# AdaLN attention and MLP block: maxima turned by VectorE, q and k split by POOL, residuals added by TensorE

## The reference, cut to what matters

```python
def _stablemax3_s(x):
    pos = 1.0 + x * (1.0 + 0.5 * x * (1.0 + x / 3.0))
    neg = 1.0 / (1.0 - x * (1.0 - 0.5 * x * (1.0 - x / 3.0)))
    return jnp.where(x >= 0, pos, neg)
...
attn = jnp.einsum('bhsd,bhtd->bhst', q, k) * scale
logits = logits - jnp.max(logits, axis=axis, keepdims=True)
s = _stablemax3_s(logits); return s / jnp.sum(s, axis=axis, keepdims=True)
...
h = _layernorm(x) * (1 + ca) + sa
x = x + ga * (attn(h) @ w_out.T + b_out)
h = _layernorm(x) * (1 + cb) + sb
x = x + gb * mlp(h)      # 128 -> 512 -> 512 -> 128, relu, weights 1 or -1
```

## Time and profile before

| | |
|---|---|
| median of 3 runs (lowest to highest) | 790.41 us (789.8 to 790.81) |
| the profiled execution's own time | 786.48 us |
| its span, first to last instruction | 784.6 us |
| granted TensorE clock, mean | 0.915 |
| DVE busy | 660.6 us (84%), 806 instructions |
| PE busy | 654.2 us (83%), 2897 instructions |
| ACT busy | 590.3 us (75%), 539 instructions |
| POOL busy | 584.9 us (75%), 348 instructions |
| chain that ended last, by engine | PE 44%, DVE 24%, issue 15%, ACT 14% |

### The profile page before, as it was taken

How to read it: one execution, slowest core, us unless ns; L and a number is a source line. 1 busy time by engine, 2 the same in 40 slices (tenths; PEclk the granted TensorE clock), 3 DMA queues, 4 the chain that set the end, 5 groups by cost and what they waited for, 6 DMA issues and landing times.

```text
span 784.6 us, 9551 instructions
## 1 busy us (share of the span) xinstructions
PE 654.2 (83%) x2897; PEld 242.1 (31%) x2897; DVE 660.6 (84%) x806; ACT 590.3 (75%) x539; POOL 584.9 (75%) x348
## 2 busy tenths in 40 slices
PE   4377777877889998899989898899879999997877
PEld 2132222222222343223322342234322342242244
DVE  6779999798989999999989998999989999985020
ACT  2036688686897889888888889888888889899411
POOL 6227697588976999589968997789967987889310
PEclk9555669677999999999999999999999999999989
DMA  4523112410233113411331123411341120001000
GB/s 147 169 77 126 42 49 81 151 50 12 64 90 129 46 49 98 155 48 50 98 117 47 48 61 83 151 48 49 85 155 48 48 78 16 8 9 45 13 18 13
DMA packets 41110, 56.35 MB, mean 72 GB/s; under 512 B 7852, under 2 KB 24516, under 8 KB 41060
## 3 DMA queue, kind: packets, MB, share of 16 engines
q1 hardware_dynamic: 40388, 54.44, 23.2%
q10 hardware_dynamic: 672, 1.31, 0.5%
HBM read 32.06 MB, written 18.89 MB: 65 GB/s over the span
## 4 chain that ended last, share of the span: by engine, by line
PE 44%; DVE 24%; issue 15%; ACT 14%; DMA 1%; ACTq 0%; DVEq 0%; POOL 0%; POOLq 0%
DVE mx L712 12%; PE MB L417 10%; DVE cub L701 9%; PE OP L499 8%; PE SA L478 8%; PE Z L458 7%; ACT prob L552 5%; ACT sq L541 5%; PE MB L426 3%; PE SA L417 2%; PE MB L391 2%; ACT hid L582 2%; PE SA L426 1%; PE MB L394 1%; PE MB L410 1%
## 5 line engine op out<-in xcount | busy, mean ns | idle before, releaser
L844 POOL TENSOR_TENSOR cub<-cub 128x2048 f32<-128x2048 f32 x128 | 460.3, 3604 | 111.4 <-DVE cub L701 111.4
L541 ACT ACTIVATE sq<-Z,shift 128x1024 f32<-128x1024 f32 x256 | 282.9, 1117 | 110.9 <-PE Z L458 108.8
L712 DVE TENSOR_REDUCE mx<-SA 128x2 f32<-128x1024 f32 (+1 forms) x278 | 307.0, 1105 | 35.9 <-PE SA L478 34.6
L701 DVE SCALAR_TENSOR_TENSOR cub<-sq,Z 128x1024 f32<-128x1024 f32 x256 | 309.5, 1210 | 12.1 <-ACT sq L541 10.8
L552 ACT ACTIVATE prob<-cub 128x2048 f32<-128x2048 f32 x128 | 244.2, 1910 | 0.0
L478 PE MATMUL SA<-KH,QL 64*128 64x512 f32 x496 | 145.7, 523 | 62.3 <-DVE mx L712 51.4
L458 PE MATMUL Z<-QH,KH 64*128 64x512 f32 x512 | 139.8, 536 | 28.9 <-DVE cub L701 28.0
L499 PE MATMUL OP<-prob,Vq 128*16 128x512 f32 x1024 | 145.1, 641 | 1.4 <-ACT OT L590 1.4
L458 PEld LDWEIGHTS Z<-QH,KH 64*128 64x128 f32 x512 | 52.5, 199 | 222.3 <-DVE cub L701 145.7
L417 PE MATMUL MB<-hid,W 128*128 128x512 f32 x216 | 119.3, 640 | 0.0
L478 PEld LDWEIGHTS SA<-KH,QL 64*128 64x128 f32 x496 | 56.6, 200 | 162.0 <-DVE mx L712 132.1
(11 more groups left out here) (113 smaller groups left out, 396.4 us busy)
## 6 DMA issues: line engine op xcount, KB each, us to landing
parts_q<-SQ SPq DMA_DIRECT2D x32, 256.0 KB, 2.6
QL<-parts_q SPq DMA_DIRECT2D x64, 128.0 KB, 2.7
QH<-parts_q SPq DMA_DIRECT2D x64, 128.0 KB, 2.8
KH<-parts_k SPq DMA_DIRECT2D x62, 128.0 KB, 2.7
parts_k<-SK SPq DMA_DIRECT2D x28, 256.0 KB, 2.6
nd<-OT SPq DMA_DIRECT2D x128, 32.0 KB
xa<-L_attn_x SPq DMA_DIRECT2D x8, 256.0 KB, 4.2
QH<-mp SPq DMA_DIRECT2D x128, 4.0 KB
```

The source lines that it names most:

```text
L541: nc.scalar.activation(sq[:, h, :], Z[:, h, :], ACT.Square, bias=shift[:, 0:1]).then_inc(s_sq, 1)
L701: nc.vector.scalar_tensor_tensor(cub[:, m % RING, h, :], sq[:, h, :], CUB_ADD, Z[:, h, :], ALU.add, ALU.mult).then_inc(s_cv, 1)
L712: nc.vector.tensor_reduce(to, unit_bank(m, u)[:, heads[0]:heads[-1] + 1, :], AX_X, ALU.max)\
L844: nc.gpsimd.tensor_tensor(ff, ff, ff, ALU.mult).then_inc(s_fp, 1)
```

## The change

1. The maxima are turned by VectorE alone: scaled by -1 and rounded into `ms`, the rest beside it, then one 32x32-block transpose into `mp`, now over 128 partitions. The three operations stand between the main ones of the quad step, the transpose behind the second cubic. TensorE's transpose, the halved maxima and the special order of `logits` go. The rows reach QH in eight DMAs of 16 pieces of 32 elements in place of four.
2. From batch 1 on ScalarE writes q and k whole into the second part's place, and POOL makes the rounded part and the rest (`parts_of`, at n = 1 and 2). k moves from place "d" to "c" of n = 1.
3. TensorE adds the residuals to x1 and y by a product with the identity; ScalarE copies the sums out. `BY_DVE` and VectorE's `take` go.
4. POOL's normalisation is x * r + (-mean * r) in place of (x - mean) * r, with two small operations to make the addend.
5. v of batch 0 moves from n = 13 to n = 2; in batch 7's steps x1, y, h2T, l0, l1_0, statistics and roots move up to one step or place earlier; in the tail l1_1 and l1_2 are spread differently. POOL's copy of V for quad 2 moves from n = 1 to n = 3.

```diff
-MISC = {b: MAIN for b in range(FIRST, B - 1)}
+MISC = {b: MAIN for b in range(B - 1)}
+MISC[FIRST] = [("hT", 1, [(0, "c", 4)]), ("q", 1, [(0, "d", 4)]), ("k", 1, [(1, "d", 4)]), ("v", 1, [(2, "c", 4)])]
...
-    ("x1", -1, [(8, "c", 4)]),
-    ("y", -2, [(9, "c", 1), (9, "d", 1), (10, "c", 1), (10, "d", 1)]),
-    ("h2T", -1, [(11, "d", 4)]),
-    ("l0_0", -1, [(12, "c", 4)]), ("l0_1", -1, [(12, "d", 4)]),
-    ("l0_2", -1, [(13, "c", 4)]), ("l0_3", -1, [(13, "d", 4)]),
-    ("l1_0", -1, [(14, "c", 1), (14, "d", 1), (15, "c", 1), (15, "d", 1)]),
+    ("x1", -1, [(8, "a", 4)]),
+    ("y", -2, [(9, "a", 1), (9, "c", 1), (9, "d", 1), (10, "a", 1)]),
+    ("h2T", -1, [(10, "d", 4)]),
+    ("l0_0", -1, [(11, "c", 4)]), ("l0_1", -1, [(11, "d", 4)]),
+    ("l0_2", -1, [(12, "c", 4)]), ("l0_3", -1, [(12, "d", 4)]),
+    ("l1_0", -1, [(13, "c", 1), (13, "d", 1), (14, "c", 1), (14, "d", 1)]),
...
-    ("l1_1", -2, [(0, "c", 4)]), ("l1_2", -2, [(2, "c", 2), (4, "d", 2)]), ("l1_3", -2, [(5, "c", 4)]),
+    ("l1_1", -2, [(0, "c", 2), (1, "d", 2)]), ("l1_2", -2, [(4, "d", 4)]), ("l1_3", -2, [(5, "c", 4)]),
...
-        mp = sb("mp", [QUAD * TB, 2, PARTS, P], F32R)
+        ms = sb("ms", [P, 2, 2, PARTS, QUAD * TB // 2], F32R)
+        mp = sb("mp", [P, 2, 2 * QUAD * TB])
...
+                pe.wait_ge(s_xbg, beta + 1)
                 for t in range(TB):
-                    mm = nc.tensor.matmul(bank4[:, t, :], num[:, t * P:(t + 1) * P], woG[:, :], start=True, stop=True)
+                    nc.tensor.matmul(bank4[:, t, :], num[:, t * P:(t + 1) * P], woG[:, :], start=True, stop=False)
+                    mm = nc.tensor.matmul(bank4[:, t, :], ident[:, :], xb[:, t, :], start=False, stop=True)
...
+                    pe.wait_ge(s_x1k, beta + 1)
                     for m in range(KC):
                         pe.wait_ge(s_taken[f"l1_{m}"], beta + 1)
                 for t in chunks:
                     for kc in range(KC):
-                        mm = nc.tensor.matmul(bank4[:, t, :], hid[1][:, kc, t * P:(t + 1) * P], W2G[:, kc, :],
-                                              start=(kc == 0), stop=(kc == KC - 1))
+                        nc.tensor.matmul(bank4[:, t, :], hid[1][:, kc, t * P:(t + 1) * P], W2G[:, kc, :],
+                                         start=(kc == 0), stop=False)
+                    mm = nc.tensor.matmul(bank4[:, t, :], ident[:, :], x1k[:, t, :], start=False, stop=True)
...
-            def maxima_across(m):
-                if 0 <= m < GROUPS and m % QUAD == QUAD - 1:
-                    pe.wait_ge(s_mx, 4 * (m + 1))
-                    nc.tensor.transpose(SA[0:QUAD * TB, 1, 0:P], mx[:, m // QUAD % 2, :], ident[:, :]).then_inc(s_mt, 1)
...
+                            if beta == 0:
+                                nc.scalar.activation(dst[:, 0, :], bank, ACT.Copy, scale=scale).then_inc(s_hi, 1)
+                            else:
+                                nc.scalar.activation(dst[:, 1, :].bitcast(F32), bank, ACT.Copy, scale=scale)\
+                                    .then_inc(s_taken[name], 1)
+                        elif name == "x1":
+                            need(act, s_x1k, beta)
+                            need(act, s_x1n, beta)
+                            nc.scalar.activation(x1[:, :, :].rearrange("p t d -> p (t d)"), bank, ACT.Copy)\
+                                .then_inc(s_taken["x1"], 1)
+                        elif name == "y":
+                            need(act, s_out, 16 * beta)
+                            nc.scalar.activation(y[:, :, :].rearrange("p t d -> p (t d)"), bank, ACT.Copy)\
+                                .then_inc(s_taken["y"], 1)
...
-            def take_maxima(m):
+                dve.wait_ge(s_a, 2 * m + u + 1)
+                to = mx[:, m // QUAD % 2, :].rearrange("p (e c) -> p e c", e=2)[:, :, TB * r + qt]
+                nc.vector.tensor_reduce(to, unit_bank(m, u)[:, :, :], AX_X, ALU.max).then_inc(s_mx, 1)
+
+            def of_maxima(m, stage):
+
                 if not (0 < m <= GROUPS and m % QUAD == 0):
                     return
                 quad = m // QUAD - 1
                 i = quad % 2
-                dve.wait_ge(s_mt, quad + 1)
-                if quad >= 2:
-                    dve.wait_ge(s_mrow[(quad - 2) % NQ], ((quad - 2) // NQ + 1) * 2 * PARTS * 16)
-                nc.vector.tensor_scalar(mp[:, i, 0, :], SA[0:QUAD * TB, 1, 0:P], -1.0, None, ALU.mult).then_inc(s_mh, 1)
-                dve.wait_ge(s_mh, quad + 1)
-                nc.vector.scalar_tensor_tensor(mp[:, i, 1, :], SA[0:QUAD * TB, 1, 0:P], -1.0,
-                                               mp[:, i, 0, :].bitcast(F32), ALU.mult, ALU.subtract).then_inc(s_mp, 1)
+                raw = mx[:, i, :].rearrange("p (e c) -> p e c", e=2)
+                if stage == 0:
+                    dve.wait_ge(s_mx, 2 * m)
+                    nc.vector.tensor_scalar(ms[:, i, :, 0, :], raw, -1.0, None, ALU.mult).then_inc(s_mh, 1)
+                elif stage == 1:
+                    dve.wait_ge(s_mh, quad + 1)
+                    nc.vector.scalar_tensor_tensor(ms[:, i, :, 1, :], raw, -1.0, ms[:, i, :, 0, :].bitcast(F32),
+                                                   ALU.mult, ALU.subtract).then_inc(s_ml, 1)
+                else:
+                    dve.wait_ge(s_ml, quad + 1)
+                    if quad >= 2:
+                        dve.wait_ge(s_mrow[(quad - 2) % NQ], ((quad - 2) // NQ + 1) * M_DMAS * 16)
+                    nc.vector.transpose(mp[:, i, :], ms[:, i].rearrange("p e a c -> p (e a c)").bitcast(F32))\
+                        .then_inc(s_mp, 1)
...
+            of_maxima(m, 0)
+            maxima(m, 0)
+            of_maxima(m, 1)
             split(b, n)
-            if s > FIRST * H:
-                take((s - 1) // H, (s - 1) % H, "cd")
             cubic(s, 1)
-            maxima(m, 1, (0, 1))
-            take(b, n, "a")
+            of_maxima(m, 2)
+            maxima(m, 1)
...
+                nc.gpsimd.tensor_tensor(nm[:, :], mv[:, :, 0], rs[:, :], ALU.mult).then_inc(s_nm, 1)
+                pool.wait_ge(s_nm, 2 * k + 1)
+                nc.gpsimd.tensor_scalar(nm[:, :], nm[:, :], -1.0, 0.0, ALU.mult, ALU.add).then_inc(s_nm, 1)
+                pool.wait_ge(s_nm, 2 * k + 2)
                 need(pool, s_free, beta)
                 for t in range(TB):
-                    last = nc.gpsimd.tensor_scalar(dst[:, t, :], src[:, t, :], mv[:, t, 0:1], rs[:, t:t + 1],
-                                                   ALU.subtract, ALU.mult)
+                    last = nc.gpsimd.tensor_scalar(dst[:, t, :], src[:, t, :], rs[:, t:t + 1], nm[:, t:t + 1],
+                                                   ALU.mult, ALU.add)
...
+            def parts_of(beta, name):
+                if beta >= B:
+                    return
+                src = SQ if name == "q" else SK
+                i = 2 * beta + "qk".index(name)
+                pool.wait_ge(s_taken[name], beta + 1)
+                nc.gpsimd.tensor_scalar(src[:, 0, :], src[:, 1, :].bitcast(F32), 1.0, 0.0, ALU.mult, ALU.add)\
+                    .then_inc(s_hi, 1)
+                pool.wait_ge(s_hi, i + 1)
+                nc.gpsimd.tensor_tensor(src[:, 1, :], src[:, 1, :].bitcast(F32), src[:, 0, :].bitcast(F32), ALU.subtract)\
+                    .then_inc(s_lo, 1)
...
-            if n in (1, 5):
-                v_in(b, 2 if n == 1 else 3)
+            if n in (1, 2) and 0 <= b < B:
+                parts_of(b + 1, "qk"[n - 1])
+            if n in (3, 5):
+                v_in(b, 2 if n == 3 else 3)
...
+                rows_g = QH[:, 2 * g:2 * g + 2, :].rearrange("p r (t k i) -> p r t k i", t=TB, k=P // 32)
                 for e in range(2):
-                    for a in range(PARTS):
-                        r = ROWS * e + R_MAX + a
-                        sp.dma_start(QH[r:r + 1, 2 * g:2 * g + 2, :].bitcast(F32), mp[2 * TB * e:2 * TB * (e + 1), quad % 2, a, :].bitcast(F32))\
+                    r = ROWS * e + R_MAX
+                    for k in range(P // 32):
+                        of = 32 * k + QUAD * TB * e
+                        sp.dma_start(rows_g[r:r + PARTS, :, :, k, :].bitcast(F32), mp[of:of + QUAD * TB, quad % 2, :])\
                             .then_inc(s_mrow[g], 16)
```

More of the change, by code:

```diff
@@ L318, in unit_before @@
             k = 2 * m + u
-            return 2 * (k - 2) if k <= FIRST_UNITS else 2 * k
-        def alone(m):
-            return m % QUAD == 0 and 2 * m >= FIRST_UNITS
+            return k - 2 if k <= FIRST_UNITS else k
         def steps(body):
@@ L465, in logits @@
                 beta, g, r, qt = logits_at(m, u)
-                if heads[0] == 0:
-                    if m == 0 and u == 0:
-                        pe.wait_ge(s_gate, 1)
-                    if m % QUAD == 0 and u == 0:
-                        pe.wait_ge(s_qk[g], (beta + 1) * LOADS * 16)
-                    need(pe, s_mx, unit_before(m, u))
-                    if m % QUAD == 0 and u == 1 and not alone(m):
```

(43 more changed lines are left out.)

52 lines of the change are left out of this document (21 added, 31 removed), and 2 rows, old and new, of the table MAIN.

## The result

The changed kernel is **slower**: 819.76 us median of four runs (817.75 to 821.36) against 790.11 for the kernel before beside it (four runs, 786.38 to 790.81), ratio 1.0384, 95% interval 1.0344 to 1.0424. The ratios of this document are formed without single slow runs (over 1.5% above the fastest of the same kernel), so they can differ a little from the ratio of the medians. The prediction of 772 us, its range and its sign were all wrong. The profiled execution has a span of 817.8 us and a mean granted clock of 0.883.

What follows compares the result with a forecast made beforehand. VectorE was taken as closest to its limit (80.37 of 85.60 us a batch), TensorE 4 us behind. -35 us plus 17 for SP's queue gave -18 from 786.48, 768.5; with 3.9 for the median, 772 us, range 753 to 787.

Steps and rivals of the forecast that it cites:

- the prediction's list: Full-clock batch, steps n = 0 to 15, mostly the larger of VectorE and TensorE: 81.0 us, 4.6 less than before.
- the price of the turning: VectorE's three small operations per quad step, on 16, 16 and 32 elements: 0.35 us together, bounds 0.25 and 0.6.
- The 4.5 us a batch from the turning: VectorE's net saving per full-clock batch from turning the maxima itself: -5.9 + 1.4 = -4.5 us.
- a rule on fixed costs: VectorE's SBUF operations pay about 150 cycles each; the three small ones would cost about 0.5 us, 0.6 more per batch.
- SP's queue: Gathers land late behind eight DMAs at n = 5; ScalarE waits 3.7 us; +2.4 us a batch, +17 in seven batches.
- the prediction's second rival: POOL becomes the bound behind the late square: 1 to 2 us more a batch, clock may drop; 780 to 787, chance 0.16.
- the first rival: The gathers are not late, so all of -35 us stays: 755 us, chance 0.20.
- Start and end: First maxima in eight DMAs make the first cubic 0.9 us later; the tail's x1 and y lengthen; together +2 us.
- "-7" for batch 0: Batch 0: -3.9 us at n = 0 to 2 and -3 at the other quads, together -7.
- "-5" for batch 1: Batch 1: same gain as batch 0 less 2 us for x1 with 16 half-clock records, -5 us.
- Sum without SP: -35 us: Whole kernel without the late gathers: -23 (batches 2 to 6) - 2 (batch 7) - 7 - 5 + 2 (start and tail).
- Normalise, "POOL has slack; I count 0": POOL's new normalisation: two small operations, about 0.4 us, against 0.2 to 0.8 for its four operations; counted as 0.

Runs made afterwards that it cites:

- 3 (both mended): Changed kernel with the scale made as a one-element maximum and SP issuing the gathers before the eight rows of maxima: 762.75 us, ratio 0.9661.
- 8 (rest later): Changed kernel with scale as one-element maximum, gathers issued first, and rest and transpose directly behind the second cubic: 751.06 us, ratio 0.9508.
- run 1: Changed kernel with the scale made as a sign-turned maximum over one element, in the same place: 791.89 us, ratio 1.0048 to the kernel before.
- 4: Kernel before with one unread 128x16 scale added on VectorE behind the first cubic of each quad step, 32 in all: 823.19 us, ratio 1.0412.
- run 5: Kernel before with an unread one-element maximum added behind the first cubic of each quad step, instead of an added scale: 791.38 us, ratio 1.0001.
- run 2: Changed kernel with SP issuing the four gathers ahead of the eight rows of maxima: 794.20 us, ratio 1.0073 to the kernel before.
- run 9: The 751.06 us version (scale as maximum, gathers first, rest and transpose behind second cubic) with x1 one place later: 751.19 us, ratio 0.9516.
- run 7: Changed kernel with the turning alone undone (TensorE's transpose, halved maxima, four DMAs as before): 783.82 us, ratio 0.9880 to the kernel before.
- run 10: The 751.06 us version with POOL normalising by subtract and multiply again, without the two small operations: 766.84 us, ratio 0.9725 to the kernel before.

## Why the prediction was wrong

Step times of the batch with number 5, n = 0 to 15, from the starts of the cubics, beside the prediction's list:

| | steps n = 0 to 15, us | sum |
|---|---|---|
| forecast | 5.2 5.0 4.8 4.8 4.8 4.9 5.4 4.85 4.9 5.7 4.85 5.4 5.4 5.0 5.0 5.0 | 81.0 |
| after | 5.0 5.9 4.5 4.7 4.7 6.6 5.3 7.1 4.9 8.8 6.3 6.1 5.0 6.2 4.8 5.0 | 90.9 |
| 3 (both mended) | 5.0 5.5 4.5 4.7 4.7 5.8 5.3 4.8 4.5 7.9 4.8 4.5 5.0 6.4 4.6 5.0 | 83.1 |
| 8 (rest later) | 5.0 5.5 4.5 4.7 4.7 5.0 5.3 4.8 4.5 6.9 4.8 4.5 5.0 6.4 4.5 5.0 | 81.3 |

- **The step that failed** is the price of the turning: "I take 0.35 us for the three (bounds 0.25 and 0.6; the transpose has no row)". The three took 1.49 + 0.35 + 0.20 = 2.04 us a quad. The price was read from a statistics operation that takes 155 ns, and the upper bound of 0.6 holds no wait at all. Neither is a bound for another kind of operation. The two small operations of the quad step before read the maxima from PSUM and ran at 0.27 us, never held. What is bounded by the nearest rows has to be near in where the operands lie, too; the true upper bound was a whole square of POOL, 3.6 us. The trace of the kernel before held a warning row, shown below this list. The Trainium skill's page on SBUF, named above, has the rule; the prediction weighed a rule on fixed costs instead and had no rival for this one.
- The 4.5 us a batch from the turning were thus given back by the lock. Runs 1 and 4 price the scale's part at 28 and 35 us, run 5 shows that it is the kind of operation, and run 8 prices the rest's part at 12 (762.75 less 751.06).
- **SP's queue** was the right mechanism at the right place: the wait of 3.2 us came where 3.7 was forecast, issues of 0.67 where 0.69 was, a landing at most 1.7 us after the last issue where 2.0 was. (The section on the anatomy of one DMA in the Trainium skill, "DMA: Bandwidth & Descriptors", which the prediction names beside this, describes DMAs issued from GpSimd; here SP issues them.) Its price was too low, 25.6 us (run 2) or 29.1 (1 against 3) for the forecast 17. Of the missing part the prediction's second rival had the cause, a late POOL, and the fallen clock, 0.94 to 0.96 in batches 2 to 6; the place is another: not the square of step 11, but that of step 9, which holds the rest.
- **The sum of the miss**, 47.8 us between 772 and 819.76: 27.9 for the scale (run 1), 29.1 less the forecast 17 for the gathers (run 3 against 1), 11.7 for the rest's place (run 8 against 3), less 3.9 because the kernel without these waits is at 751.06 and not at the 755 of the first rival.
- **The list of steps** itself held once both were out of the way: 81.3 against 81.0 us. It was right by sum and not row by row, which is in part luck. Steps 9 and 13 take 1.2 and 1.4 us more than listed, step 1 takes 0.5: in 9 VectorE idles 0.94 us for TensorE's x1 (and where that is moved away, the lock takes the same time, run 9), in 13 the rest is held by POOL for 1.0. Steps 8, 11, 12 and 14 take 0.4 to 0.9 less.
- **Start and end.** "-7" for batch 0 measured -6.1 (84.4 to 78.3 in run 8), "-5" for batch 1 -4.5; batches 2 to 6 together -21.3 for -23. Batch 7 took 4.0 longer instead of 2 less, and the tail 5.5 less instead of more. The first cubic came 0.2 us later, not 0.9. So "Sum without SP: -35 us" has -33.2 as its measured counterpart (the two profiled executions), or -39 by the medians; that it is so near is partly luck, since batch 7 and the tail missed by about 6 and 7 us, in opposite directions. At the start of the changed kernel the first rows of maxima landed at most 1.1 us after their last issue, where 2.4 was counted, and its first cubic came at 46.8 instead of 48.3.
- **Normalise, "POOL has slack; I count 0"**, was no zero but a gain: one operation costs 0.45 instead of 0.79 us, and in the kernel of run 8 that is worth 16 us (run 10). In the changed kernel as it stands this was not measured.
- That VectorE's relief is worth nothing where TensorE ends the step was right (run 7).
- **Open:** the spread of run 7 (773.83 to 786.87) has no explanation here, and how the 16 us of run 10 divide between the lock and the fallen clock was not measured: the steps show 1.7 us at n = 13 and 0.5 to 3.4 us at n = 15, in four batches.

The warning row stands in the start of the kernel before, ahead of the first batch:

```profile
9.26 1.90 POOL L832 TENSOR_SCALAR W<-prob 128x2048 f32<-128x2048 uint8 x1 [2.00 <-DMA prob<-L_ffn_k]
...
10.18 1.06 DVE L661 TENSOR_SCALAR mod<-mod 128x8 f32<-128x8 f32 x2
```

These are two scales of 8 columns from SBUF to SBUF. The first takes 1.00 us and ends 0.03 us after POOL's instruction, the second 0.16 us.
